# A lag of three groups for the scores of a graph attention layer, with four tiles of maxima and narrower turned denominators

## The reference, cut to what matters

```python
xl = (x @ W_l + b_l).reshape(n, HEADS, C)
xr = (x @ W_r + b_r).reshape(n, HEADS, C)
e = (edge_attr @ W_e).reshape(-1, HEADS, C)
g = jax.nn.leaky_relu(xl[src] + xr[dst] + e, NEG_SLOPE)
logits = jnp.einsum('ehc,hc->eh', g, att)
amax = jax.ops.segment_max(logits, dst, num_segments=n)
ex = jnp.exp(logits - amax[dst])
denom = jax.ops.segment_sum(ex, dst, num_segments=n)
alpha = ex / (denom[dst] + 1e-16)
out = jax.ops.segment_sum(xl[src] * alpha[..., None], dst, num_segments=n)
```

## Time and profile before

| | us |
|---|---|
| median of three runs | 6530.24 |
| lowest and highest | 6523.35, 6541.23 |
| profiled execution | 6528.89 |
| its span | 6527.2 |
| mean granted TensorE clock, share of full | 0.68 |
| busy in the span: PE, DVE, ACT, POOL | 3615.7, 3719.8, 1769.3, 3543.2 |

### The profile page before, as it was taken

The page is one execution under the profiler, slowest core; times in us unless marked ns, Lnnn a source line. Parts: engine busy times, 40 slices in busy tenths (PEclk is TensorE's granted clock), DMA queues, the critical chain, the costliest instruction groups (busy, mean ns, idle before and its releaser), DMA issues. The chain is left out here.

```text
span 6527.2 us, 58257 instructions
## 1 busy us (share of the span) xinstructions
PE 3615.7 (55%) x12150; PEld 2056.4 (32%) x12150; DVE 3719.8 (57%) x4301; ACT 1769.3 (27%) x3305; POOL 3543.2 (54%) x3662
## 2 busy tenths in 40 slices
PE   3565656573444544444444434676767667677662
PEld 2344434331222222222222212333333333333331
DVE  9978955552333333333333333777777777777776
ACT  1233323361111111111111111333333333333332
POOL 4430033326666666666666656666666666666653
PEclk8566667675666666666776655767676776766765
DMA  8756467613343344333333312333333333333331
GB/s 195 205 188 201 150 159 199 108 30 88 98 101 101 101 100 101 102 101 100 100 102 99 101 41 62 84 86 83 87 85 85 85 85 86 85 87 84 86 82 32
DMA packets 1376052, 678.01 MB, mean 104 GB/s; under 512 B 1051533, under 2 KB 1254927, under 8 KB 1374994
## 3 DMA queue, kind: packets, MB, share of 16 engines
q1 hardware_dynamic: 1099684, 341.45, 22.5%
q0 software_dynamic: 116880, 124.33, 10.0%
q10 hardware_dynamic: 159390, 211.24, 9.4%
HBM read 344.06 MB, written 332.55 MB: 104 GB/s over the span
## 5 line engine op out<-in xcount | busy, mean ns | idle before, releaser
L1650 POOL DMA_INDIRECT got<-tabg,ix x1568 | 1483.1, 946 | 892.8 <-DMA t<-rows 442.4
L1456 POOL DMA_INDIRECT got<-tabg,ix x1568 | 1483.0, 946 | 825.1 <-issue 436.7
L1476 PE MATMUL p_inter<-hid,W 128*128 128x512 f32 x392 | 388.9, 1094 | 1230.7 <-DVE run L1562 1031.5
L1554 DVE TENSOR_TENSOR_SCAN own<-mk,own,p_first 128x512 f32<-128x512 bf16 x195 | 248.8, 1276 | 1426.7 <-remote 762.7
L177 PE MATMUL p_out<-ident,run 128*128 128x128 f32 (+1 forms) x3136 | 688.5, 369 | 171.8 <-DVE run L493 66.3
L177 PEld LDWEIGHTS p_out<-ident,run 128*128 128x128 f32 (+1 forms) x3136 | 572.2, 218 | 531.7 <-issue 416.4
L1785 DVE TENSOR_TENSOR_SCAN top<-p_reset,top,logit 128x512 f32<-128x512 f32 x195 | 249.5, 1280 | 575.4 <-DMA tops<-top 263.2
L163 PE MATMUL p_small<-ident,ea 128*32 128x128 f32 (+1 forms) x784 | 176.1, 370 | 712.9 <-ACT rows L1748 660.4
L1476 PEld LDWEIGHTS p_inter<-hid,W 128*128 128x128 f32 x392 | 95.4, 302 | 1274.6 <-issue 1108.9
L1508 ACT ACTIVATE gate<-p_gate,BF 128x512 f32<-128x512 f32 x196 | 134.8, 688 | 1059.7 <-issue 807.8
L493 DVE TENSOR_TENSOR_SCAN run<-p_mk,run,feat 128x512 f32<-128x512 f32 x302 | 370.4, 1268 | 63.5 <-remote 42.0
(11 more groups left out here) (347 smaller groups left out, 6749.5 us busy)
## 6 DMA issues: line engine op xcount, KB each, us to landing
t<-rows ACTq DMA_DIRECT2D x195, 512.0 KB
first<-start SPq DMA_DIRECT2D x780, 128.0 KB
t<-rows ACTq DMA_DIRECT2D x195, 288.0 KB
got<-tabg,ix POOLq DMA_INDIRECT x3136
start<-zeros SPq DMA_DIRECT2D x100, 500.0 KB
ea<-in_ea_dram SPq DMA_DIRECT2D x390, 128.0 KB
mk<-marks SPq DMA_DIRECT2D x780, 64.0 KB
start<-zeros SPq DMA_DIRECT2D x195, 256.0 KB
```

Source lines behind the costliest of these rows:

```text
L1456: nc.gpsimd.indirect_dma_start(got[s][0:g.p, cc, h, :], None, tabg, bass.IndirectOffsetOnAxis(ap=ix[0:g.p, g.n, h, cc:cc + 1], axis=0)).th ...
L1476: nc.tensor.matmul(p_inter[s][:, 0:g.w], W2[:, :], hid[s][:, 0:g.w], start=True, stop=True).then_inc(mixed, 1)
L1650: nc.gpsimd.indirect_dma_start(got[s][0:g.p, cc, h, :], None, tabg, bass.IndirectOffsetOnAxis(ap=ix[0:g.p, g.n, h, cc:cc + 1], axis=0)).th ...
```

## The change

The number of maxima tiles becomes TOPS = 4. Score, maximum, exponents, exps and accumulate go to lag 3; turn_back, small_back, to_rows and store to lag 4; keep_logits to lag 2; store_top to lag 6. rs gets a step and a semaphore of its own, load_resets with lag 1, and load waits for turned_ea where it waited for resets. The denominators are turned by four products with every sixteenth column of the identity (eight columns), where four full transposes stood, and ACT reads the 32 values without gaps.

```diff
-    R = 2 * HEADS
+    R, TOPS = 2 * HEADS, 4
...
-        top = [sb(c, f"top{i}", [P, 1 + W]) for i in range(2)]
+        top = [sb(c, f"top{i}", [P, 1 + W]) for i in range(TOPS)]
...
                 def load(g):
                     s, row = g.slot(AHEAD), snapped(sp, g.row)
-                    wait_from(sp, resets, g.n - AHEAD + 1)
                     wait_from(sp, owned, g.n - AHEAD + 1)
+                    wait_from(sp, turned_ea, g.n - AHEAD + 1)
...
-                    sp.dma_start(rs[s][:, 0:g.w], marks[0][:, 1, ds(row, g.w)]).then_inc(first_in[s], 16)
+
+                def load_resets(g):
+                    s = g.slot(AHEAD)
+                    wait_from(sp, resets, g.n - AHEAD + 1)
+                    sp.dma_start(rs[s][:, 0:g.w], marks[0][:, 1, ds(snapped(sp, g.row), g.w)]).then_inc(rs_in[s], 16)
...
-                each_group(sp, (0, load), (5, store_top))
+                each(sp, (0, load), (1, load_resets), (6, store_top))
...
-                    pe.wait_ge(first_in[s], 80 * g.turn(AHEAD) + 80)
+                    pe.wait_ge(first_in[s], 64 * g.turn(AHEAD) + 64)
...
                     wait_from(pe, featured, g.n)
-                    wait_from(pe, drained_small, g.n - 2)
+                    wait_from(pe, drained_small, g.n - 3)
...
-                    if g.it is not None or g.base + 2 <= NG:
-                        pe.wait_ge(featured, g.n + 3)
+                    if g.it is not None or g.base + 3 <= NG:
+                        pe.wait_ge(featured, g.n + 4)
...
-                    turn_to_edges(nc, p_small[:, :].rearrange("p (c q) -> p c q", c=C), den[g.slot(2)], g, ident).then_inc(smalls, 1)
+                    for cc in range(C):
+                        mm = nc.tensor.matmul(p_small[0:g.p, cc * R:(cc + 1) * R], by_place(den[g.slot(2)], g)[:, :, cc], ident[:, 0:P:HC], start=True, stop=True)
+                    mm.then_inc(smalls, 1)
...
+                    pe.wait_ge(rs_in[g.slot(AHEAD)], 16 * g.turn(AHEAD) + 16)
                     wait_from(pe, falls, g.n)
...
-                each_group(pe, (2, score), (1, add_edge_terms), (0, first_rows), (3, turn_back), (3, small_back), (0, gathered_rows), (0, edge_rows))
+                each(pe, (3, score), (1, add_edge_terms), (0, first_rows), (4, turn_back), (4, small_back), (0, gathered_rows), (0, edge_rows))
...
-                each_group(act, (2, exps), (1, fifths), (3, to_rows), (3, store), (0, their_rows), (0, edge_rows), (1, keep_logits))
+                each(act, (3, exps), (1, fifths), (4, to_rows), (4, store), (0, their_rows), (0, edge_rows), (2, keep_logits))
...
-                    s = g.slot(2)
-                    wait_from(dve, tops_out[s], 16 * g.turn(2))
+                    s, m = g.slot(2), g.slot(TOPS)
+                    wait_from(dve, tops_out[m], 16 * g.turn(TOPS))
...
-                each_group(dve, (2, maximum), (2, exponents), (1, attend), (0, spread), (1, leak), (2, accumulate))
+                each(dve, (3, maximum), (3, exponents), (1, attend), (0, spread), (1, leak), (3, accumulate))
```

More of the change, by code:

```diff
@@ L1598, in edges_4 @@
         zeroed, made, weights_in = (sem(c, n) for n in ("zeroed", "made", "weights_in"))
-        first_in, got_in, mk_in = ([sem(c, f"{n}{i}") for i in range(AHEAD)] for n in ("first_in", "got_in", "mk_in"))
-        stored, tops_out = ([sem(c, f"{n}{i}") for i in range(2)] for n in ("stored", "tops_out"))
+        first_in, got_in, mk_in, rs_in = ([sem(c, f"{n}{i}") for i in range(AHEAD)] for n in ("first_in", "got_in", "mk_in", "rs_in"))
+        stored = [sem(c, f"stored{i}") for i in range(2)]
+        tops_out = [sem(c, f"tops_out{i}") for i in range(TOPS)]
         (resets, turned_first, turned_ea, turned_got, featured, gotten, summed_ea, owned, added, leaked, scored,
@@ L1605, in edges_4, with each @@
                                 "decayed", "weighted", "summed", "dens", "rowed", "smalls", "drained", "drained_small"))
+        def each(eng, *steps):
+            run_ticks(eng, 0, NG + 1 + max(lag for lag, _ in steps), steps, 3 * AHEAD)
         with nc.Block() as block:
@@ L1622, in load @@
                         sp.dma_start(mk[s][h * D:(h + 1) * D, 0:g.w], marks[0][h, 0:1, ds(row, g.w)].to_broadcast((D, g.w))).then_inc(mk_in[s], 16)
-                    sp.dma_start(rs[s][:, 0:g.w], marks[0][:, 1, ds(row, g.w)]).then_inc(first_in[s], 16)
+                def load_resets(g):
+                    s = g.slot(AHEAD)
+                    wait_from(sp, resets, g.n - AHEAD + 1)
+                    sp.dma_start(rs[s][:, 0:g.w], marks[0][:, 1, ds(snapped(sp, g.row), g.w)]).then_inc(rs_in[s], 16)
                 def store_top(g):
-                    s = g.slot(2)
+                    s = g.slot(TOPS)
                     sp.wait_ge(maxed, g.n + 1)
                     sp.dma_start(tops[:, ds(snapped(sp, g.row), g.w)], top[s][0:P:HC, 1:1 + g.w]).then_inc(tops_out[s], 16)
-                each_group(sp, (0, load), (5, store_top))
-                for s in range(2):
-                    sp.wait_ge(tops_out[s], 16 * ((NG + 2 - s) // 2))
+                each(sp, (0, load), (1, load_resets), (6, store_top))
+                for s in range(TOPS):
+                    sp.wait_ge(tops_out[s], 16 * ((NG + TOPS - s) // TOPS))
             @block.gpsimd
@@ L1734, in exps @@
                         wait_from(act, lefts, g.n)
-                        nc.scalar.activation(top[1 - s][:, 0:1], top[s][:, W:W + 1], ACT.Copy).then_inc(carried, 1)
+                        nc.scalar.activation(top[(g.base + 1) % TOPS][:, 0:1], top[g.slot(TOPS)][:, W:W + 1], ACT.Copy).then_inc(carried, 1)
                     act.wait_ge(falls, g.n + 1)
@@ L1746, in to_rows @@
                     act.wait_ge(smalls, g.n + 1)
-                    small = p_small[0:g.p, :].rearrange("p (c h a f) -> p c h a f", h=2, a=HEADS, f=HC)
+                    small = p_small[0:g.p, 0:C * R].rearrange("p (c h a) -> p c h a", h=2, a=HEADS)
                     nc.scalar.activation(rows[s][0:g.p, :, :, D:D + HEADS].rearrange("p h c f -> p c h f"),
-                                         small[:, :, :, :, 0], ACT.Copy).then_inc(drained_small, 1)
+                                         small, ACT.Copy).then_inc(drained_small, 1)
                 def store(g):
@@ L1784, in maximum @@
                     dve.wait_ge(resets, g.n + 1)
[L1785 to L1786 removed]
+                    nc.vector.tensor_tensor_scan(top[m][:, 1:1 + g.w], p_reset[:, 0:g.w], logit[s][:, 0:g.w],
+                                                 NEG if g.zero else top[(g.base - 1) % TOPS][:, W:W + 1], ALU.add, ALU.max).then_inc(maxed, 1)
                 def exponents(g):
[L1790 removed]
+                    s, m = g.slot(2), g.slot(TOPS)
                     dve.wait_ge(maxed, g.n + 1)
[L1792 removed]
+                    nc.vector.tensor_tensor(p_logit[s][:, 0:g.w], p_logit[s][:, 0:g.w], top[m][:, 1:1 + g.w], ALU.subtract).then_inc(shifted, 1)
                     wait_from(dve, carried, g.n)
[L1794 removed]
+                    nc.vector.tensor_tensor(p_reset[:, 0:g.w], top[m][:, 0:g.w], p_reset[:, 0:g.w], ALU.add).then_inc(lefts, 1)
                     dve.wait_ge(lefts, g.n + 1)
                     wait_from(dve, decayed, g.n - 1)
[L1797 removed]
+                    nc.vector.tensor_tensor(expo[s][:, 0:g.w], p_reset[:, 0:g.w], top[m][:, 1:1 + g.w], ALU.subtract).then_inc(falls, 1)
                 def spread(g):
```

1 line of the change is left out of this document (removed).

## The result

The changed kernel takes 6554.75 us (median of 7 executions, 6547.18 to 6571.33), the kernel before on the same chip 6527.24 us (7 executions, 6516.9 to 6541.23). The ratio is 1.0044, 95% interval 1.0034 to 1.0055: 27.5 us slower. The forecast was 6535 us with a range of 6450 to 6625; the time lies in the range, 20 us above the point, and the difference of 27.5 us (0.4%) is past the 0.3% under which I had said that nothing could be told.

A forecast was written before the change was run, and what follows sets the result against it. POOL's gathers plus a late turned_got update were taken as the bound, 12.12 us a tick. 6528.9 + 8.5 - 4 = 6533.4 us; that execution being 1.3 us under the median, the forecast was 6535, range 6450 to 6625.

The forecast's parts named there:

- Case A: Forecast case for the attention layer: POOL and the late PE update bound the tick; 6535 us, own range 6525 to 6550, chance 0.42.
- Only the last term can be won: POOL's tick is 8 x 0.947 + 7 x 0.30 + 2.4 = 12.1 us; only the 2.4 us wait for turned_got is winnable.
- While POOL issues gathers, updates of PE come through late: In the attention layer, turned_got was said to reach POOL some 2.2 us after a group's last gather.
- My test for being wrong at the root: Wrong if POOL's wait follows PE's turning of the rows, or ticks after the last gather grow by much more than one.
- One more tick, +8.5: After the last gather, the longer lags add one tick of 8.54 us.
- The start, -4: At the layer's start, POOL's long wait of 8.63 us may shrink by 0 to 8.3 us; half was taken.
- Lags and four maxima tiles, 0: In the steady tick, lags cost nothing; the maximum's 263.2 us of store waits go without gain; bounds 0 and -263.
- Resets loaded apart, 0, bounds 0 to +1.28 us a tick: SP's loads start 1.28 us later in the tick, behind rs and the store; taken as no effect.
- Eight-column products, 0, bounds 0 to -1.27 us of PE a tick: PE's four denominator products stream 8 columns instead of 128, weight loads staying; any saving lies inside POOL's wait.
- B: Rival, faster: PE's update slips through before a group's gathers end; -67.7 us of POOL idle time, 6467 us, chance 0.23.
- C: Rival, faster: DVE's start, held by the store of the maxima, is in the loop; 263 us go, 6272, chance 0.11.
- D: Rival, slower: SP's later loads delay PE's updates, lengthening the wait before each group's first gather; 6624 or 6778 us, chance 0.24.

The follow-up runs named there:

- e7_products_twice: The kernel before with the denominators turned by eight-column products issued twice over, eight a group; 6627.69 us, ratio 1.0147.
- e6_turns_again_2: The changed kernel with the denominators turned by four full transposes again, on the chip with late news; 6545.71 us, ratio 1.0020 to the kernel before.
- e10_resets_apart: The kernel before with only SyncE's order changed, the resets loaded apart one group behind the other loads; 6534.12 us, ratio 1.0016.
- e11_products_alone_2: The kernel before with only the eight-column products for the denominators, on the chip with late news; 6540.82 us, ratio 1.0023.
- e9_after_half: The changed kernel with half of layer 4's gathers left out, four a group instead of eight; 5914.84 us, ratio 0.9063 to the kernel before.
- e3_four_tops: The kernel before with only four maxima tiles instead of two, on the chip where nothing waits; 5559.30 us, ratio 0.9994.
- e5_changed_again: The changed kernel itself, unaltered, on the faster chip; 5562.86 us against 5561.2 for the kernel before, ratio 1.0006.

## Why the prediction was right or wrong

The time lies in the range and the account of the bound held, but the 20 us above the point are no scatter. Case A's own range ended at 6550, and two of its signs did not come: first to last gather is 20.3 us above 2375 where 15 were allowed, and the products into p_small got longer. What was missed, 21.4 us in the steady ticks, comes from parts that I had put at 0. That they stayed small enough for the range is owed to the wait that covers them, whose room I had not measured; to that extent the number was lucky.

**What bounds the kernel: right.** Halving the gathers of this layer gave 650 us; on the chip with the news on time the wait is gone. "Only the last term can be won" held for the changed kernel too, and the changed kernel lost in that term alone. What I could not know from one trace is that another chip lacks the term.

**"While POOL issues gathers, updates of PE come through late": too wide.** The trace of the kernel before contradicts it as it stands. Timeline of the kernel before, where gathers run from 5005.76 on:

```profile
5006.55 1.92 PE L1705 MATMUL p_logit<-act_in,AT 128*128 128x512 f32 x2
...
5008.50 0.60 ACT L1759 ACTIVATE logit<-p_logit 128x512 f32<-128x512 f32 x1 [1.07 <-issue]
```

ACT takes the finished product of the scores 0.03 us after its end. From group 15 on ACT was idle ahead of this step in 157 ticks, and in all 157 it went on within 0.1 us. What comes late every time are the turned denominators and turned_got: ACT took the former 2.2 us or more after their end in all 175 ticks in which it was idle. In the start it differs again: ACT used the turned rows at 4016.58 while POOL's gather of 4016.33 was running, so the news does not need a pause of POOL there. What singles out these two steps, and whether the update leaves late or the modelled ends of PE's records are early, no run here shows. The forecast needs only turned_got to be late, so the account of the bound stands.

**My test for being wrong at the root** was that POOL's wait follows PE's turning. In the kernel before it does not. Pushed far enough, it does (e7_products_twice). The right form is a maximum of two moments, and I should have written down the distance to the second.

**One more tick, +8.5: right, a little high.** Measured +8.1 in the changed kernel, 180.8 - 174.9 = +5.9 in e6_turns_again_2.

**The start, -4: wrong in its place, and smaller.** In the changed kernel POOL's long wait is 9.73 us, not shorter than the 8.63 of the earlier trace rows. The group after it does not wait at all (0.30 us), and the next one 3.46. In sum the first 15 groups take 1.1 us less than before.

```profile
4051.19 0.95 POOL L1659 DMA_INDIRECT got<-tabg,ix  x1 [9.73 <-DMA mk<-marks]
```

**Lags and four maxima tiles, 0: right in sign and as mechanism.** The 263.2 us of store wait were renamed, as said under A. With everything but the products in place (e6_turns_again_2) the gathers still took 10.9 us longer, 4.4 of which SyncE's order shows alone; the other 6.5 us belong to lags and tiles together, or to the scatter of single executions. That was not separated: four maxima tiles alone ran only on the chip on which nothing waits, and the lags alone on neither.

**Resets loaded apart, 0, bounds 0 to +1.28 us a tick: nearly right.** e10_resets_apart puts it at 6.6 / 195 = 0.03 us a tick by its medians, at the low end of the bounds. An interval of 5 to 16 us says that the order is not quite free. The section that I cited from the Trainium skill ("DMA: Bandwidth & Descriptors", "Issuing engines are not separate DMA queues") says on which DMA engines the transfers of all issuing engines run. It says nothing of the order in which one engine issues them, so that a changed order costs nothing was my own conclusion and not its rule.

**Eight-column products, 0, bounds 0 to -1.27 us of PE a tick: this is the step that failed.** I wrote that they stream 8 columns instead of 128 and "the loads of their weights stay". The columns did shrink to 8. The loads did not stay: they doubled in number, and each got longer. PE's time for them grew from 146.1 / 196 = 0.75 us to 368.8 / 196 = 1.88 us a tick, +1.13 where the bound allowed at most 0. The reason stood in the earlier trace rows: L1705 has 392 records for 196 products, two for each product of 32-bit values, while the transposes into p_small have 784 records for 784. In these traces a transpose is one record, a product of the same 32-bit operands two, each with its own load of the weights. Even the price of such a load stood in the trace of before, a median of 332 ns for the products of L1705 where the transposes have 212. In the changed kernel it is 330. At 8 columns the loads span the whole time, 1.94 us of them beside 1.92 us of products in the tick shown above; that they are what limits it is my reading, no run varied the columns. The Trainium skill, "TensorE: Matmul & The Clock Gate", section "Terms", mentions a transpose mode that is faster for FP32; the trace agrees in direction, with 0.75 us against 1.88 for the same four blocks. Here are the rows of loads: those of L1705 and of the transposes into p_small in the kernel before, and those of the changed kernel's L1710:

```profile
L1705 PEld LDWEIGHTS p_logit<-act_in,AT x392: 186/332/338, 4008.1 to 6392.0; 128*128 128x128 f32 x196
```

```profile
L177 PEld LDWEIGHTS p_small<-ident,den x784: 152/212/230, 4055.8 to 6399.7; 128*128 128x128 f32 x195, 128*40 128x40 f32 x1
```

```profile
L1710 PEld LDWEIGHTS p_small<-ident,den x1568: 149/330/337, 4064.6 to 6433.0; 128*128 128x128 f32 x195, 128*40 128x40 f32 x1
```

I then costed this edit at nothing because the pause covers it. That cover was real but not whole: 222.7 us more of products came out as 9 to 13 us (e11_products_alone_2). They are not all that PE gained: from 4100 to 6300 us it is busy 1820.4 us instead of 1511.3, or 1.8 us more a tick, and the 0.7 us beyond the products come with a granted clock of 0.65 instead of 0.70. The longer pause in it is spread over all ticks, also over those in which PE had turned early, so crossing the second limit does not explain it; why the news comes 0.05 us later (2.50 instead of 2.45) with more work on PE stays open. Doubled, the cover is gone in 74 ticks, and 97 us come out.

**The rivals.** B did not come: no group of the changed kernel after group 7 shows 0.30 us ahead of its first gather. C is refuted by e6_turns_again_2 and e9_after_half. D named the right place, the wait ahead of a group, and its mark of 2.6 us was just met (2.61, start included), but mostly for another reason: products on PE, of which D said nothing. The sum of what was shown where the news is late, in the gathers of single executions: 9.1 us for the products, 4.4 for SyncE's order and 6.8 not separated make the 20.3 us, and the last tick adds 8.1, against 27.5 measured.

None of the kernels that do the whole work beats the kernel before. The best, e3_four_tops, has an interval that holds 1.

## What to carry to other kernels

Count records before pricing a product: here a 32-bit product that only moves data has two records with two weight loads, a transpose one, and going from 128 columns to 8 did not make up for that (1.88 us instead of 0.75). Where an edit hides under another engine's wait, write down how many microseconds of cover there are and what takes over when they are used up: here the first ones went almost without a trace in the time, and past the edge POOL's wait followed PE's turning. And before a wait is tuned, see whether another chip has it at all.

## What the runs showed that I had not expected

Two chips run the same program in 5561 and 6527 us, each steady within about 0.6%. On the slower one, in the steady ticks, news of PE's turned denominators and turned rows reaches ACT and POOL only some 2.2 us or more after POOL's last gather of a group (3.97 us late in the tick shown), on the faster one within 0.04 us in the tick shown, under the same gathers. What in the chip or its surroundings makes the difference isn't shown. TensorE's granted clock differs too: in the middle of the stage the changed kernel has 0.66 on the one and 0.76 on the other. The gathers' rate, 945 ns with 0.30 us between two, is the same on both.

Window of e5_changed_again on the faster chip:

```profile
4500.00:4700.00 200.00, 177.01 (x623) 110.19 (x622) 176.63 (x201) 84.96 (x181) 151.21 (x160) 0.76 0.47 104
```

The eight-column products also came with a lower granted clock: 0.72 before, 0.66 in the changed kernel, 0.65 with the products alone, in the same stretch. With the products issued twice it was 0.71 again, at 178.27 us of PE. The long stretch from 4100 to 6300 us says the same: 0.70 before, 0.65 changed, 0.66 with the products alone, 0.71 with them twice. Longer, denser work did not keep the clock down; the runs don't say what did.

```profile
4900.00:5100.00 200.00, 165.59 (x510) 95.69 (x509) 145.92 (x164) 70.30 (x147) 122.71 (x131) 0.65 0.38 84
```

```profile
4900.00:5100.00 200.00, 178.27 (x624) 119.36 (x624) 139.78 (x158) 69.32 (x144) 120.03 (x127) 0.71 0.37 83
```

(The first is e11_products_alone_2, the second e7_products_twice.)
